# Delta recurrence with its operands exchanged, and masked decays moved to GpSimd

## The chip, the core and the metric

The kernel runs on one core of one Trainium2 chip. A core has five engines that run side by side and meet only at semaphores: TensorE (PE, matrix products, whose weight loads the profile keeps apart as PEld), VectorE (DVE), ScalarE (ACT), GpSimd (POOL) and the queue that starts transfers (SP). The metric is the device time of one execution in microseconds (us); lower is better.

## The reference, cut to what matters

The input is four sequences of 1024 tokens of 128 numbers. First comes one layer of a gated delta recurrence with six heads, keys of 128 and values of 32 numbers:

```python
def step(S, inp):                      # S: batch, head, 128 x 32
    q_t, k_t, v_t, g_t, b_t = inp
    S = S * jnp.exp(g_t)[..., None, None]
    corr = jnp.einsum('bhk,bhkv->bhv', k_t, S)
    u = (v_t - corr) * b_t[..., None]
    S = S + k_t[..., None] * u[:, :, None, :]
    o_t = jnp.einsum('bhk,bhkv->bhv', q_t, S)
    return (S, o_t)
S, o = lax.scan(step, S0, (qt, kt, vt, gt, bt))
```

Behind it come six layers of windowed attention (16 heads of 64, windows of 32 tokens) with a feed-forward block each, all in float32.

## The kernel before, in words

`delta_layer` walks the 1024 tokens in eight tiles of 128, all four sequences (NB = 4) at once. A tile is one block of the program, with a barrier behind it. It first makes projections, convolutions and norms, and then takes the six heads in three pairs; x = 0, 1 is the head of a pair.

The tile's 128 recurrence steps are done as matrices. For a head, k·kᵀ weighted by decays gives a triangular A (`weigh`, into `am`), which TensorE turns (`turn_a`, L384) and ScalarE copies (`take_at`: four copies of 32 rows into `atc`, L638, and a whole one into `at`, L640). The inverse of I + A is doubled block by block in six levels (i = 1 to 6). In each level TensorE makes `first_products`, ScalarE copies them (`p1`, L690 or L694), TensorE makes `second_products`, and VectorE subtracts and turns them (L945, L947; L926 in the last two levels). Between first and second products of levels 1 to 4, TensorE makes the decays and the k·kᵀ, k·q products of the next pair (`decay`, L366 and L367; `products`). A decay reads `gm`, a masked matrix that `masked_decay` on VectorE makes at the start of a pair (L877).

Behind the levels comes what this document calls the pair's closing:

1. `L503`, `L505`: k and q times the state, per sequence one product each; VectorE makes the right side r from them (L972 to L976);
2. `turn_a` for the next pair;
3. `L517`: the inverse (`tt`) times r gives u; VectorE takes it twice (L981, L982);
4. `L525`, `L527`: u times `pm` and times `kt` give the output and the change of the state; VectorE adds both (L990 to L994);
5. `turn_k` for the next pair (L390), which waits for `at`.

The last pair of a tile has no steps 2 and 5. In all products of steps 1, 3 and 4 the loaded operand (the first argument) has 128 columns and the moving one has 32:

```python
pe.matmul(p[3 * x][:, b * DV:(b + 1) * DV], act_qkv[:, H1 + h, s], state[:, h, b, :], start=True, stop=True)
```

`at_block(b)` is the slice of 32 partitions that begins at 32·b. The program gives a product whose operands have 32 or 64 rows or columns a part of TensorE's array; in the trace the form behind the names (`32*32`, `64*32`, `128*128`) is rows by columns of the loaded operand's tile. A float32 product stands in the trace as two records (x2), a turn as one.

`local_layers` is a pipeline over steps g, in an order that is written out for each engine. In VectorE's list `ffn(t, 0)` adds the finished attention output of a tile to `y` (L1581), `sums` reduces squares (L1520), and TensorE's first output product of the next tile (L1287) waits for that addition, since both use one bank.

Of the kernel before, what the change touches and what calls it, by code (L numbers as in the profile page):

```python
# [15 lines left out]
ALU = mybir.AluOpType  # L16
ACT = mybir.ActivationFunctionType
# [121 lines left out]
def delta_layer(nc, sbuf, names, p, y, msk, ident, ones, cst, c, cols, load_done, init_done,  # L139
# [3 lines left out]
    with ExitStack() as ctx:  # L143
# [41 lines left out]
        u = sb("u", [P, 2, 2, NB, DV])  # L185
        o = sb("o", [P, NB, VD])
# [11 lines left out]
        def at_block(n):  # L198
# [20 lines left out]
         on_ready, on_turned, ot_ready, wo_ready, x1_ready, x1_stored) = names(  # L219
            "ks_ready", "r_ready", "u_ready", "u_taken", "o_ready", "s_ready", "o_done", "om_ready",  # L220
            "ostd_ready", "on_ready", "on_turned", "ot_ready", "wo_ready", "x1_ready", "x1_stored")
# [35 lines left out]
        for t in range(-1, NT + 1):  # L257
            attend, behind, ahead = 0 <= t < NT, t >= 1, t + 1 < NT
            LAST_LN, NEXT_LN = 1, 1 + behind
            with nc.Block(no_gpsimd_drain=True) as block:  # L260
# [12 lines left out]
                def _(pe):  # L273
# [119 lines left out]

                    def first_products(pair, i, n):

                        for x in range(2):
                            pe.wait_ge(t_ready, n[x])
                            if i == 1 and pair:
                                pe.wait_ge(r_ready, 2 * pair - 1 + x)
# [26 lines left out]
                    def second_products(pair, i, n):  # L426

                        for x in range(2):
                            pe.wait_ge(p1_taken, n[x])
                            if i == 1 and pair:  # L430
                                pe.wait_ge(u_taken, 2 * pair - 1 + x)
                                pe.wait_ge(s_ready, 2 * pair - 1 + x)
# [7 lines left out]
                            elif i == SMALL:  # L440
                                for b in range(NB):
# [39 lines left out]
                    for pair in range(H1 // 2):  # L481
                        heads = (2 * pair, 2 * pair + 1)

                        for i in range(1, LEVELS):
                            n = [pair * 2 * (LEVELS - 1) + 2 * (i - 1) + x + 1 for x in range(2)]
                            first_products(pair, i, n)
                            if pair + 1 < H1 // 2 and 1 <= i <= 4:
# [12 lines left out]
                        for x, h in enumerate(heads):  # L500
                            for b in range(NB):
                                s = slice(b * P, (b + 1) * P)
                                pe.matmul(p[3 * x][:, b * DV:(b + 1) * DV], act_qkv[:, H1 + h, s],  # L503
                                          state[:, h, b, :], start=True, stop=True)
                                last = pe.matmul(p[3 * x][:, P + b * DV:P + (b + 1) * DV], act_qkv[:, h, s],  # L505
                                                 state[:, h, b, :], start=True, stop=True)
                            last.then_inc(ks_ready, 1)
                        if pair + 1 < H1 // 2:
                            for x in range(2):
                                turn_a(2 * pair + 2 + x)  # L510
                        for x, h in enumerate(heads):
# [4 lines left out]
                            for b in range(NB):  # L516
                                last = pe.matmul(p[3 * x + 1][:, b * DV:(b + 1) * DV], tt[:, x, b, :],  # L517
# [1253 lines left out]
```

## Time and profile before

| | |
|---|---|
| median of 3 runs | 5441.72 us (5439.07 to 5442.9) |
| the profiled execution | 5437.88 us, span 5435.9 us |
| granted TensorE clock, mean | 0.884 |
| busy: PE, DVE, ACT, POOL | 89%, 69%, 51%, 39% of the span |
| one tile of the delta layer | 238.56 us (its `xin` load is issued at 976.25, that of the next at 1214.81) |
| the six local layers | from 1952 us to 5418 us |

The profiled execution lies inside the range of the three runs. A busy share says how long an engine had work in flight, so that TensorE at 89% may still be waiting in places and may be loaded far below its rate in others; which of the two holds in a stretch is read from the timeline of that stretch. The delta layer is the first 14 of the page's 40 slices.

### The profile page before, as it was taken

What the parts mean: (1) busy time and instruction counts of PE and PEld (TensorE: products, weight loads), DVE (VectorE), ACT (ScalarE), POOL (GpSimd) and SP (SyncE); (2) the same over time, 40 slices, a digit from 0 to 9 for tenths busy, and PEclk for the clock granted to TensorE, in tenths of its full rate; (3) what the DMA queues carried; (4) which work ended last, traced back from release to release, by engine and by line L of the source; (5) the groups of instructions that cost most, each with busy time, mean ns of one, the idle gap of its engine ahead of it and who ended that gap; (6) DMA issues with size and microseconds to landing.
All of it is one profiled execution on the core that took longest, in us unless ns stands there. A gap on an engine that the chain in (4) does not pass through costs nothing. (4 is left out here: it accounts for less than half of the span.)

```text
span 5435.9 us, 193069 instructions
## 1 busy us (share of the span) xinstructions
PE 4820.7 (89%) x82128; PEld 3000.6 (55%) x82128; DVE 3747.0 (69%) x6340; ACT 2797.1 (51%) x5325; POOL 2115.8 (39%) x2244
## 2 busy tenths in 40 slices
PE   5867778686777769999999999999999999999997
PEld 3746657474655735555555555555555555555554
DVE  5454554636455468878788888787877888888774
ACT  4243342424334236666666666666666666666664
POOL 2121121212112135555555555555555555555551
PEclk8676776767676669999999999999999999999999
DMA  0000000000000012222222322233222322232222
GB/s 23 4 3 5 2 5 2 5 4 3 6 2 3 2 59 70 67 61 75 73 68 68 82 72 62 64 79 77 68 62 68 79 68 68 74 78 66 59 62 65
DMA packets 255938, 253.45 MB, mean 47 GB/s; under 512 B 29680, under 2 KB 248816, under 8 KB 254704
## 3 DMA queue, kind: packets, MB, share of 16 engines
q1 hardware_dynamic: 255088, 241.09, 17.6%
q8 instruction: 658, 10.78, 0.8%
q14 instruction: 192, 1.57, 0.1%
HBM read 29.71 MB, written 4.19 MB: 6 GB/s over the span
## 5 line engine op out<-in xcount | busy, mean ns | idle before, releaser
L1468 POOL TENSOR_TENSOR turn<-prod 128x512 f32<-128x512 f32 x768 | 982.2, 1279 | 1393.4 <-DVE prod L1508 1371.1
L1205 PE MATMUL banks<-w2s,xs 128*128 128x512 f32 x2304 | 1185.8, 597 | 37.7 <-DVE xs L1541 30.2
L1508 DVE TENSOR_TENSOR prod<-banks,tabs 128x1024 f32<-128x1024 f32 x768 | 940.1, 1224 | 335.2 <-PE banks L1205 322.2
L1477 POOL TENSOR_TENSOR turn<-turn,rs 128x512 f32<-128x512 f32 x768 | 794.8, 1056 | 285.8 <-ACT rs L1371 285.8
L1239 PEld LDWEIGHTS banks<-msk,turn 128*128 128x128 f32 x3072 | 352.5, 140 | 479.8 <-issue 380.6
L1520 DVE TENSOR_REDUCE ss<-sq 128x8 f32<-128x512 f32 x768 | 493.4, 677 | 11.6 <-ACT sq L1353 9.9
L1353 ACT ACTIVATE sq<-banks 128x512 f32<-128x512 f32 x768 | 456.4, 594 | 54.7 <-DVE prod L1508 20.8
L1239 PE MATMUL banks<-msk,turn 128*128 128x128 f32 x3072 | 471.6, 276 | 4.1 <-ACT qt L1386 2.3
L1287 PE MATMUL banks<-ot,w2s 128*128 128x512 f32 x768 | 430.7, 643 | 34.7 <-DVE y L1581 34.0
L1386 ACT ACTIVATE qt<-banks 128x512 f32<-128x512 f32 x384 | 229.2, 597 | 421.5 <-PE banks L1239 420.7
L1384 ACT ACTIVATE kx<-banks 128x512 f32<-128x512 f32 x384 | 229.3, 597 | 407.6 <-PE banks L1239 407.1
L1264 PEld LDWEIGHTS banks<-v,pt 64*32 64x32 f32 x24576 | 269.0, 105 | 289.7 <-ACT qt L1386 141.7
L1393 ACT ACTIVATE pt<-banks 128x512 f32<-128x512 f32 x384 | 229.3, 597 | 324.4 <-PE banks L1246 324.3
L1205 PEld LDWEIGHTS banks<-w2s,xs 128*128 128x128 f32 x2304 | 348.6, 191 | 53.6 <-DVE xs L1541 31.7
L1545 DVE TENSOR_REDUCE mx<-banks 128x8 f32<-128x512 f32 x384 | 263.5, 686 | 130.1 <-PE banks L1225 120.1
L1264 PE MATMUL banks<-v,pt 64*32 64x66 f32 x24576 | 332.5, 225 | 0.2 <-issue 0.2
L1225 PE MATMUL banks<-kx,qt 64*32 64x64 f32 x24576 | 326.0, 222 | 0.0
L1275 PEld LDWEIGHTS banks<-msk,att 128*128 128x128 f32 x1536 | 161.1, 140 | 282.2 <-DVE att L1559 280.6
L1225 PEld LDWEIGHTS banks<-kx,qt 64*32 64x32 f32 x24576 | 299.6, 105 | 0.1
L1314 PE MATMUL banks<-xf,w2s 128*128 128x512 f32 (+1 forms) x576 | 289.8, 616 | 3.1 <-DVE xf L1599 2.8
L831 DVE SCALAR_TENSOR_TENSOR cv<-pre,cw,cv 128x512 f32<-128x512 f32 x336 | 238.3, 781 | 76.9 <-ACT cv L593 71.4
L1559 DVE TENSOR_TENSOR att<-banks,rc 128x512 f32<-128x512 f32 x384 | 265.5, 691 | 13.2
(217 smaller groups left out, 8398.9 us busy)
## 6 DMA issues: line engine op xcount, KB each, us to landing
v<-v_tok SPq DMA_DIRECT2D x1152, 132.0 KB
v<-v_tok SPq DMA_DIRECT2D x384, 66.0 KB
v<-v SPq DMA_DIRECT2D x188, 132.0 KB, 2.5
w2s<-in_weights SPq DMA_DIRECT2D x10, 768.0 KB, 4.9
tabs<-in_rot SPq DMA_DIRECT2D x40, 128.0 KB, 3.2
w2s<-in_weights SPq DMA_DIRECT2D x1, 2713.5 KB, 11.1
w2s<-in_weights SPq DMA_DIRECT2D x10, 256.0 KB, 3.0
xin<-in_x SPq DMA_DIRECT2D x8, 256.0 KB, 2.8
```

The source lines that it names most:

```text
L1205: pe.matmul(a_bank(use), xs[:, t % 2, b * P:(b + 1) * P], w[:, at:at + 512], start=True, stop=True).then_inc(a_done, 1)
L1225: last = pe.matmul(sc[n * WIN:(n + 1) * WIN, h, b * 2 * WIN:(b + 1) * 2 * WIN], qt[r, j, b * P + n * WIN:b * P + (n + 1) * WIN], kx[r, j, ...
L1239: last = pe.transpose(turn_bank[:, i * P:(i + 1) * P], src[:, i * P:(i + 1) * P], ident)
L1264: last = pe.matmul(pv[n * WIN:(n + 1) * WIN, h, b, :], pt[r, g % 2, b * P + n * WIN:b * P + (n + 1) * WIN], v2[r, h2, b, n, i * DV1:(i + 1 ...
L1287: pe.matmul(out_bank, w[:, W_O + j * P:W_O + (j + 1) * P], ot[:, g % 3, :], start=(j == 0), stop=(j == NP2 - 1)).then_inc(o_done, 1)
L1314: pe.matmul(a_bank(n)[0:r, :], w[:, at:at + r], xf[:], start=True, stop=True)\
L1353: a.activation(sq[:, r % 2, :], a_bank(use), ACT.Square).then_inc(sq_done, 1)
L1468: gp.tensor_tensor(turn[:, r % ROTS, :, :].rearrange(halves, s=2), prod[:, r % 2, 0, :, :].rearrange(halves, s=2), prod[:, r % 2, 1, :, :] ...
L1477: gp.tensor_tensor(turn[:, r % ROTS, :, :], turn[:, r % ROTS, :, :], along(rs[:, q % 2, b, :], DH), ALU.mult).then_inc(rot_done, 1)
L1508: v.tensor_tensor(prod[:, r % 2, :, :, :], a_bank(use).rearrange("p (h d) -> p h d", h=HU).unsqueeze(1) .to_broadcast([P, 2, HU, DH]), tab ...
L1520: v.tensor_reduce(ss[:, q % 2, b, :], sq[:, r % 2, :].rearrange("p (h d) -> p h d", h=HU), AX.X, ALU.add).then_inc(red_done, 1)
L1559: v.tensor_tensor(att[:, g % 2, :, :, :].rearrange("p b h n -> p h b n"), pv[:, :, :, 0:DH], rc[:].unsqueeze(3).to_broadcast([P, 2, NB, DH ...
```

## The change

Four things are edited in the delta layer, and one line is moved in the local layers.

- **Exchanged operands.** In steps 1, 3 and 4 the 32-column operand is loaded and the 128-column one moves. The result of sequence b stands in the 32 partitions of `at_block(b)`, turned. ScalarE copies it to SBUF (`kst`, `ut`, `ost`), and TensorE turns it back, all four sequences in one turn. k and q are moved by one product of 256 columns.
- **State products earlier.** k and q times the state are made in level 1, turned back in level 2, and taken by VectorE behind level 3 (`rests`). They need the state of the tile before, and no result of the levels.
- **Masked decays.** Those of heads 2 to 5 are made by POOL, two heads ahead, one instruction of 128 by 512 for a head.
- **ScalarE's copies.** `atc` and `at` are split into `take_blocks` and `take_at`, with the copies of `ut` ahead and those of `ost` between them.
- **Local layers.** VectorE's `ffn(t, 0)` stands ahead of the two `sums` of its step.

```diff
+                    def state_products(pair):
+                        for x in range(2):
+                            h = 2 * pair + x
+                            if pair:
+                                pe.wait_ge(s_ready, h - 1)
+                            for b in range(NB):
+                                last = pe.matmul(p[3 * x + 1][at_block(b), 0:2 * P], state[:, h, b, :],
+                                                 act_qkv[:, h:h + H1 + 1:H1, b * P:(b + 1) * P],
+                                                 start=True, stop=True, skip_group_check=True)
+                            last.then_inc(ks_ready, 1)
+                    def turn_state_products(pair):
+                        for x in range(2):
+                            pe.wait_ge(kst_taken, 2 * pair + x + 1)
+                            for i in range(2):
+                                last = pe.transpose(p[3 * x + 1][:, (2 + i) * P:(3 + i) * P], kst[:, x, i, :], ident)
+                            last.then_inc(ks_turned, 1)
...
                             first_products(pair, i, n)
+                            if i == 1:
+                                state_products(pair)
+                            elif i == 2:
+                                turn_state_products(pair)
...
                             for b in range(NB):
-                                last = pe.matmul(p[3 * x + 1][:, b * DV:(b + 1) * DV], tt[:, x, b, :],
-                                                 r1[:, x, 2, b, :], start=True, stop=True)
-                            last.then_inc(u_ready, 1)
+                                last = pe.matmul(p[3 * x][at_block(b), 0:P], r1[:, x, 2, b, :], tt[:, x, b, :],
+                                                 start=True, stop=True, skip_group_check=True)
+                            last.then_inc(ut_ready, 1)
+                        if pair + 1 < H1 // 2:
+                            for x in range(2):
+                                turn_a(2 * pair + 2 + x)
+                        for x, h in enumerate(heads):
+                            pe.wait_ge(ut_taken, h + 1)
+                            pe.transpose(p[3 * x][:, P:2 * P], ut[:, x, :], ident).then_inc(u_ready, 1)
...
+                                pe.matmul(p[3 * x + 2][at_block(b), 0:P], u[:, x, 0, b, :], pm[:, h % 4, b, :],
+                                          start=True, stop=True, skip_group_check=True)
+                            for b in range(NB):
+                                last = pe.matmul(p[3 * x + 2][at_block(b), P:2 * P], u[:, x, 1, b, :],
+                                                 kt[:, x, b, :], start=True, stop=True, skip_group_check=True)
+                            last.then_inc(ost_ready, 1)
+                        for x, h in enumerate(heads):
+                            pe.wait_ge(ost_taken, h + 1)
+                            for i in range(2):
+                                last = pe.transpose(p[3 * x + 1][:, i * P:(i + 1) * P], ost[:, x, i, :], ident)
                             last.then_inc(o_ready, 1)
...
+                    def masked_decay(h):
+                        g.wait_ge(g_ready, 1)
+                        g.wait_ge(decay_ready, h - 1)
+                        g.tensor_tensor(gm[:, h % 2, :, :], over_batches(gt), along(t24[:, 0, :, h], P), ALU.mult)\
+                            .then_inc(gm_ready, 1)
...
+                            if i == 3:
+                                rests(heads)
...
+                        if 8 <= g and g % 8 == 1:
+                            ffn(g // 8 - 1, 0)
                         if feed:
                             sums(g, 0)
                             sums(g, 1)
-                        if 8 <= g and g % 8 == 1:
-                            ffn(g // 8 - 1, 0)
```

TensorE's order in the closing of a tile's first pair, before (semaphores that a row waits for in brackets):

```order
L503 MATMUL banks<-state,act_qkv 128x32
L505 MATMUL banks<-state,act_qkv 128x32
...
L384 MATMUL banks<-msk,am 128x128 [waits pm_ready,a_ready]
L384 MATMUL banks<-msk,am 128x128 x3
L517 MATMUL banks<-r,tt 128x32 [waits upper_spread,r_ready,lower_spread,tri_ready]
L517 MATMUL banks<-r,tt 128x32 x3
...
L525 MATMUL banks<-u,pm 128x32 [waits pm_ready,kt_ready,u_taken]
L527 MATMUL banks<-u,kt 128x32
...
L390 MATMUL banks<-msk,act_qkv 128x128 [waits at_ready]
L390 MATMUL banks<-msk,act_qkv 128x128 x3
```

and in the changed kernel (L535 is the product for u, L543 its turn, L549 and L552 the products with `pm` and `kt`, L558 their turns):

```order
L535 MATMUL banks<-tt,r 32x128 [waits upper_spread,r_ready,lower_spread,tri_ready]
L535 MATMUL banks<-tt,r 32x128 x3
...
L389 MATMUL banks<-msk,am 128x128 [waits pm_ready,a_ready]
L389 MATMUL banks<-msk,am 128x128 x3
L543 MATMUL banks<-msk,ut 128x128 [waits ut_taken] x2
L549 MATMUL banks<-pm,u 32x128 [waits pm_ready,kt_ready,u_taken]
L549 MATMUL banks<-pm,u 32x128 x3
L552 MATMUL banks<-kt,u 32x128 x4
...
L558 MATMUL banks<-msk,ost 128x128 [waits ost_taken]
L558 MATMUL banks<-msk,ost 128x128
...
L395 MATMUL banks<-msk,act_qkv 128x128 [waits at_ready]
```

The state products have left the closing; each other group keeps its place, and two groups of turns, each behind a copy by ScalarE, have come in.

TensorE's order in level 1 of the first pair of the changed kernel, where the state products (L406) now stand between the first products (L430) and the next pair's decay (L371, L372):

```order
L430 MATMUL banks<-tc,ao 32x32 [waits ao_ready,t_ready]
L430 MATMUL banks<-tc,ao 32x32 x15
L406 MATMUL banks<-act_qkv,state 32x256 x8
L371 MATMUL banks<-msk,gm 128x128 [waits pm_ready,gm_ready,kt_ready]
L372 MATMUL banks<-gm,msk 128x128
```

Eight products of 256 moving columns stand there, where sixteen of 32 stood in the closing.

ScalarE's order in the closing of the first pair, of the changed kernel:

```order
L750 ACTIVATE ut<-banks 128x128 [waits ut_ready] x2
L668 ACTIVATE atc<-banks 32x128 [waits ao_ready,a_turned]
L668 ACTIVATE atc<-banks 32x128 x3
L668 ACTIVATE atc<-banks 32x128 [waits ao_ready,a_turned]
L668 ACTIVATE atc<-banks 32x128 x3
L756 ACTIVATE ost<-banks 128x256 [waits ost_ready] x2
L673 ACTIVATE at<-banks 128x512 [waits a_turned] x2
L685 ACTIVATE kt<-banks 128x512 [waits ktok_ready] x2
```

Before, the copies of `at` stood directly behind those of `atc`, with nothing ahead or between; now `at` stands behind both copies of `ost`.

## Rows read from the trace of the kernel before

**Rows 1.** The page's second part, clock over 40 slices.
```profile
PEclk8676776767676669999999999999999999999999
```

**Rows 2.** Stretches: us, busy PE, PEld, DVE, ACT, POOL (x), PEclk, DMA, GB/s.
```profile
1103.84:1124.40 20.56, 20.56 (x97) 20.23 (x96) 7.79 (x29) 3.82 (x11) 3.48 (x8) 0.50 0.01 1
1124.40:1153.95 29.55, 22.47 (x690) 20.47 (x689) 13.29 (x42) 7.53 (x21) 3.01 (x8) 0.79 0.01 3
```

**Rows 3.** Timeline, first pair's closing: start us, us, instructions, [idle before].
```profile
1103.84 0.63 PE L503 MATMUL banks<-state,act_qkv 128*128 128x32 f32 x2
1103.95 0.42 DVE L926 TENSOR_SCALAR tt<-banks 64x256 f32<-64x256 f32 x1 [0.68 <-PE banks L455]
...
1110.69 1.95 PE L384 MATMUL banks<-msk,am 128*128 128x128 f32 x8
...
1111.82 1.11 ACT L638 ACTIVATE atc<-banks 32x128 f32<-32x128 f32 x4 [9.07 <-PE banks L384]
...
1112.43 3.46 PE L517 MATMUL banks<-r,tt 128*128 128x32 f32 x16
...
1114.22 0.29 DVE L981 COPY u<-banks 128x128 f32<-128x128 f32 x1 [2.17 <-PE banks L517]
...
1115.70 0.61 PE L525 MATMUL banks<-u,pm 128*128 128x32 f32 x2
...
1119.34 0.29 DVE L990 TENSOR_TENSOR o<-o,banks 128x128 f32<-128x128 f32 x1 [0.81 <-PE banks L527]
...
1122.53 1.95 PE L390 MATMUL banks<-msk,act_qkv 128*128 128x128 f32 x8
...
1124.40 1.08 PE L405 MATMUL banks<-tc,ao 32*32 32x32 f32 x64
```

**Rows 4.** Timeline, last pair of the same tile, its closing.
```profile
1193.42 1.97 PE L455 MATMUL banks<-tt,p 64*64 64x64 f32 x16
...
1195.32 0.63 PE L503 MATMUL banks<-state,act_qkv 128*128 128x32 f32 x2
...
1213.23 0.29 DVE L994 TENSOR_TENSOR state<-state,banks 128x128 f32<-128x128 f32 x1
```

**Rows 5.** Timeline, turns and wide products at two clock levels.
```profile
1069.09 1.07 PE L384 MATMUL banks<-msk,am 128*128 128x128 f32 x8 [1.97 <-DVE pm L906]
...
1127.28 0.64 PE L366 MATMUL banks<-msk,gm 128*128 128x128 f32 x2
1127.71 0.63 PE L367 MATMUL banks<-gm,msk 128*128 128x128 f32 x2
```

**Rows 6.** Timeline, local layers, products on 64-row, 32-column tiles.
```profile
3004.82 0.84 PE L1225 MATMUL banks<-kx,qt 64*32 64x64 f32 x64
...
3005.59 1.12 PE L1287 MATMUL banks<-ot,w2s 128*128 128x512 f32 x2
```

**Rows 7.** By line: xcount | busy us, mean ns | idle before, releasers.
```profile
L733 POOL TENSOR_TENSOR sq<-act_qkv 128x512 f32<-128x512 f32 x96 | 109.5, 1149 | 164.6 <-PE banks L356 163.6
L366 PE MATMUL banks<-msk,gm 128*128 128x128 f32 x384 | 107.4, 374 | 59.3 <-DVE pm L906 57.1 <-DVE gm L877 1.1
...
L690 ACT ACTIVATE p<-banks 128x128 f32<-128x128 f32 x240 | 66.6, 278 | 229.2 <-PE banks L405 141.9 <-PE banks L413 83.6
...
L694 ACT ACTIVATE p<-banks 64x256 f32<-64x256 f32 x48 | 18.2, 379 | 61.8 <-PE banks L421 61.4
```

**Rows 8.** Timeline, VectorE inside a doubling level.
```profile
1082.80 0.29 DVE L945 TENSOR_TENSOR tc<-tc,banks 128x128 f32<-128x128 f32 x1 [2.95 <-PE banks L437]
```

**Rows 9.** Timeline, the local layers' step behind a finished tile.
```profile
3013.73 1.10 PE L1287 MATMUL banks<-ot,w2s 128*128 128x512 f32 x2 [0.61 <-DVE y L1581]
...
3016.14 0.63 ACT L1403 ACTIVATE e<-e 128x512 f32<-128x512 f32 x1 [0.24 <-DVE e L1549]
...
3017.46 0.86 PE L1264 MATMUL banks<-v,pt 64*32 64x66 f32 x64
```

**Rows 10.** Group by line, all layers: the output products and their waits.
```profile
L1287 PE MATMUL banks<-ot,w2s 128*128 128x512 f32 x768 | 430.7, 643 | 34.7 <-DVE y L1581 34.0 <-ACT ot L1399 0.7
```

More of the change, by code:

```diff
@@ L185, in delta_layer @@
         u = sb("u", [P, 2, 2, NB, DV])
+        kst = sb("kst", [P, 2, 2, P])
+        ut = sb("ut", [P, 2, P])
+        ost = sb("ost", [P, 2, 2, P])
         o = sb("o", [P, NB, VD])
@@ L500, in _ @@
                         for x, h in enumerate(heads):
[L501 to L511, printed above, removed]
                             pe.wait_ge(tri_ready, h + 1)
@@ L679, in _ @@
                     for h in range(2):
+                        take_blocks(h)
+                    for h in range(2):
                         take_at(h)
@@ L695, in _ @@
                                         .then_inc(p1_taken, 1)
+                            if i == 1:
+                                for x in range(2):
+                                    a.wait_ge(ks_ready, 2 * pair + x + 1)
+                                    a.activation(kst[:, x, :, :], blocks(p[3 * x + 1][:, 0:2 * P], 2), ACT.Copy)\
+                                        .then_inc(kst_taken, 1)
                             if i == SMALL:
@@ L707, in _ @@
                                     rstd(NEXT_LN, p[6])
+                        for x in range(2):
+                            a.wait_ge(ut_ready, 2 * pair + x + 1)
+                            a.activation(ut[:, x, :], p[3 * x][:, 0:P], ACT.Copy).then_inc(ut_taken, 1)
+                        if more:
+                            for x in range(2):
+                                take_blocks(2 * pair + 2 + x)
+                        for x in range(2):
+                            a.wait_ge(ost_ready, 2 * pair + x + 1)
+                            a.activation(ost[:, x, :, :], blocks(p[3 * x + 2][:, 0:2 * P], 2), ACT.Copy)\
+                                .then_inc(ost_taken, 1)
                         if more:
@@ L757, in _ @@
                             last.then_inc(lower_spread, 1)
+                        if pair + 2 < H1 // 2:
+                            g.wait_ge(lower_spread, 2 * pair + 2)
+                            for x in range(2):
+                                masked_decay(2 * pair + 4 + x)
+                    g.wait_ge(gm_ready, H1)
                     g.wait_ge(ao_ready, H1 * (SMALL - 1))
@@ L935, in _ @@
                         more = pair + 1 < H1 // 2
-                        if more:
-                            masked_decay(2 * pair + 2)
-                            masked_decay(2 * pair + 3)
                         for i in range(1, LEVELS):
```

51 lines of the change are left out of this document (26 added, 25 removed).

## The prediction, made before the changed kernel ran

> **What bounds the kernel now.** I read the slices first. The granted clock lies at 5 to 8 tenths in the first 14 slices, which are the delta layer, and at 9 behind them [rows 1]: the two layers have different limits. Next come stretches of one tile of the delta layer (t = 4), taken from its timeline. The closing of its first pair is 20.56 us long and TensorE is busy for all of it, at a granted clock of 0.50; in the levels behind it TensorE is busy for 22.47 of 29.55 us at 0.79 [rows 2]. So in the closing TensorE itself sets the time, and at the lower of its two levels, 1.2 GHz.
>
> Then the timeline of the closing, for what TensorE does there [rows 3]. The sixteen products of step 1 take from 1103.84 to 1110.69, 6.85 us or 0.428 us each. Eight turns take 1.74 us (1110.69 to 1112.43), 0.217 each. The eight products of step 3 end at about 1115.70 (3.27 us), the sixteen of step 4 at 1122.53 (6.83 us), and eight more turns at 1124.40. The price of 0.428 us is the point: the decay's products, which move 128 columns through a full tile, also stand 0.43 us apart at this level (1127.28 to 1127.71) [rows 5]. A product that moves 32 columns and one that moves 128 cost the same, so the loading of 128 columns is what is paid for in steps 1, 3 and 4. The last pair's closing has no turns for a next pair: from 1195.32 until VectorE's last row ends at 1213.52 (1213.23 + 0.29), 18.20 us [rows 4].
>
> **What the exchange does to a product.** Each now loads 32 columns and moves 128 (256 for the state). If products on the four column tiles went one behind the other, each would still cost 0.43 us, by its moving columns. If the four sequences' products run side by side, four cost what one does. No row shows a tile of 128 rows and 32 columns. The nearest are the local layers' score products on tiles of 64 rows and 32 columns: 64 records from 3004.82 until TensorE's next work at 3005.59, 0.77 us [rows 6]. One record that moves 64 columns takes 0.119 us of its tile at the low level (16 records from 1193.42 to 1195.32) [rows 4], so about 0.06 at the full one; 64 of them would take 3.8 us in a row, and 1.9 us if only the two row halves overlapped. They take 0.77: column tiles of one row group do overlap. I take full overlap, 0.43 us for a group of four at the low level, and as the other end no overlap, 1.71 us.
>
> **The closing, worked out anew**, with 1103.84 as zero, at the low level, and about 0.2 us from a product's end to its reader. Head 0's u products run from 0 to 0.43. Head 1's wait for VectorE's last block of `tt`, which starts at 1103.95 and takes 0.42 [rows 3]: 0.65 to 1.08. Eight turns (`turn_a`) run to 2.82. The turns of `ut` follow to 3.26; ScalarE copied it at 0.28 us each [rows 7] before that. VectorE takes u, two instructions like that of 0.29 us [rows 3], which overlap a little, 0.5 us for a head: 3.25 to 3.75 and to 4.25. The products with `pm` and `kt`, two groups of four for a head, run from 3.85 to 4.70 and to 5.56. ScalarE is in `take_blocks` from 2.15 to 4.4 (two times 1.11 us [rows 3]), which is just over before `ost` is ready at 4.9. It copies `ost` at 0.38 us [rows 7], by 5.3 and 6.15. TensorE turns the two at 5.56 to 6.0 and 6.3 to 6.7. ScalarE's whole copies `at` now come behind, about 0.6 us each, to 7.35, so that `turn_k` runs from 6.85 to 8.6, and the next pair's first products begin there. Before, they began at 20.56 (1124.40) [rows 3]. The closing shrinks by 12.0 us. VectorE fits `first_t`, output and state into 4.25 to 8.4, by its rows of 0.29 us [rows 3].
>
> In the last pair the same chain without the turns gives u taken by 2.0 and 2.65, products from 2.15 to 3.87, turns until 5.0, and the state's last row by 6.3, against 18.20: 11.9 us less.
>
> **What comes in elsewhere**, per pair:
> - State products in level 1: two heads, each one group of 256 moving columns, 0.86 us at the low level, 1.7 us in all. TensorE is between `first_products` and the decay there, and ScalarE's copies of `p1` are done before the decay is, so this is on the path. Against it, the levels' clock of 0.79 [rows 2] means that it rises somewhere in them, and it may rise sooner behind the wide products; the turns show what the two levels differ by (eight in 1.07 us [rows 5] against 1.74). I take 1.3 us; the ends are 0.9 and 1.7.
> - Four turns in level 2, 0.87 us at the low level, half at the high one: 0.7.
> - `rests` on VectorE, eight instructions of 0.29 us, 2.3 us. They fall into the idle time of a level, 2.95 us [rows 8]. Nothing, if that cover holds; without it 2.3 us. The levels of the last pair are shorter, and 0.5 us may show there.
> - ScalarE's copies of `kst`, 0.38 us each: beside the decay's products. Nothing.
> - The masked decays: TensorE waited for VectorE's `gm` for 1.1 us in the whole program [rows 7], so their leaving VectorE is worth at most that. On POOL one costs about 1.15 us, by the nearest form, a 128 by 512 product of two operands [rows 7], a pair ahead of its reader. Nothing.
> - Waits that I haven't seen and changes of tile form: 0.5.
>
> So a pair gives 12.0 − 1.3 − 0.7 − 0.5 = 9.5 us. The L366 row counts its products in 384 records, eight for a head [rows 7]: 48 heads, 24 pairs. 24 times 9.5 is 228 us. The profiled execution's 5437.88 us less 228 is 5210; the median of the runs shown stands 3.84 us above that execution, so 5214 us.
>
> **The line moved in the local layers.** TensorE waits 34.0 us in total for the addition at L1581 [rows 10], 0.61 us in the step shown [rows 9]. The addition now comes about 1.2 us earlier and that wait goes. But the step is then VectorE's: its list has the same work up to the subtraction of the maxima, ScalarE's exponent starts only behind that (3016.14, released by VectorE), and TensorE's L1264 at 3017.46 needs a copy that stands behind this exponent [rows 9]. What is late next is the same thing as before. I take 0; the ends are 0 and −34 us.
>
> **The rivals.**
> - *No overlap* (slower). The loads are the reason it could be: the groups load into tiles that share all four row groups. Ten groups of four (four for the state, two for u, four for output and state) cost 1.71 instead of 0.43 us, 12.8 us more in a pair, and 9.5 us less becomes 3.3 more. 24 times 3.3 is 79, so 5521 us. It decides from 1.38 us for a group on (0.43 + 9.5/10), an overlap of less than 1.24. The 64-row tiles speak against it [rows 6]; for it speaks only that no 128-row tile is in the trace. The Trainium skill has this as a rule (TensorE: Matmul & The Clock Gate, Part 3: Packing small matmuls): a weight load overlaps with products in flight only when their row groups differ, and here none do. The score products, with two row groups and 0.77 us for 64 records, don't agree with it as far as it would forbid column tiles; the same part's table measures three column tiles at 2.38 times, which would leave most of the gain, as an estimate.
> - *Half overlap*: 0.85 us for a group, 4.3 us more in a pair, 5.2 us less than before. 5442 − 125 = 5317 us. 64 records in 0.77 us are 12 ns each, so that a limit on issue does not bind groups of eight long records.
> - *The clock rises*. The old closing stood at 0.50 although TensorE was busy throughout [rows 2]; elsewhere in the same tile TensorE does reach the high level, as at the turns at 1069.09 [rows 5]. If the new closing and level 1 run at 2.4 GHz, the turns in the closing cost 0.87 us less twice over, the turns and products 0.8, and the state products and the first decay 1.5: about 3.2 us in a pair at the chain's links that are TensorE's, 77 us in all, 5137 us. Against it: the new closing has gaps at each copy, and half of TensorE's work in it is turns.
> - *The moved line pays in full*: 34 us more, 5180 us.
>
> **How the numbers follow.** Full overlap near the clock of before: 0.60, 5214 us. Clock rises: 0.19, 5137. Half overlap: 0.09, 5317. No overlap: 0.07, 5521. Moved line pays: 0.05, 5180. A measurement of this kernel can tell 0.2%, some 11 us, from no change. Only the case without overlap is slower, and no case but a mixture of poor overlap and lost cover lies within 0.2%: faster 0.92, same 0.01, slower 0.07. The range leaves out the two poor cases (0.16) and a little of the best: below, the risen clock, 5137, with some margin left out of it; above, a pair's gain cut by the uncovered `rests` (2.3) and state products at their dearer end (0.4), 65 us more than 5214. That is 5140 to 5285.
>
> **What would show it.** In the changed kernel's timeline: four products of one head on 128*32 tiles start within some tens of ns, and a group takes about 0.43 us at 0.50; the closing of a first pair is 8 to 9 us long, with ScalarE's copy of `ost` behind `take_blocks` by less than 0.5 us; level 1 is 1 to 2 us longer; no idle time of TensorE is put down to `r` in level 5 or to POOL's `gm`; the local layers' stretch keeps its length while L1287's wait for L1581 is gone. The prediction is wrong if products of one group start one behind the other, if the clock in the closing isn't 0.50, or if levels 1 to 4 grow by more than 3 us.

## The result, and the profile after

The changed kernel takes 5142.47 us (median of 4 runs, 5140.68 to 5147.27) against 5440.93 us for the kernel before beside it (4 runs, 5439.07 to 5442.90). The ratio is 0.9453, with a 95% interval of 0.9436 to 0.9469. It is faster by 298 us. The forecast was 5214, with a range of 5140 to 5285: the time lies inside, at the very low end, and the gain was under-forecast by 72 us.

First the page of the changed kernel: span, busy time by engine and the granted clock in 40 slices.

```profile
span 5138.7 us, 192901 instructions
...
PE 4539.0 (88%) x81984; PEld 2649.1 (52%) x81984; DVE 3693.6 (72%) x6212; ACT 2844.3 (55%) x5469; POOL 2152.4 (42%) x2276
...
PEclk8777777777777899999999999999999999999999
```

Beside [rows 1], the slices of the delta layer all stand at 7 or 8 now, where many stood at 6, and the layer is about a slice shorter. How the time divides is read from the first instruction behind the delta layer, SyncE's load of the key mask. It starts at 1952.26 us in the profile of before. In that of the changed kernel:

```profile
1683.46 0.35 SPq L1167 DMA_DIRECT2D sq<-in_key_mask  x1
```

The delta layer became 268.8 us shorter (forecast 228), and what is behind it, up to the end of the span, 28.4 us shorter: 3483.6 before, 5138.7 − 1683.46 = 3455.2 now (forecast 0). The two add up to the 297.2 us between the spans. So both terms of the forecast were too small, one by 41 us and one by 28.

**The same tile of the delta layer** (t = 4), by stretches, with the columns of [rows 2]: the levels and the closing of the first pair, then those of the second.

```profile
1142.16:1173.28 31.12, 24.09 (x710) 21.10 (x709) 14.31 (x45) 8.29 (x23) 5.65 (x12) 0.77 0.01 3
1173.28:1181.10 7.82, 7.26 (x71) 5.01 (x71) 4.59 (x17) 4.83 (x15) 3.64 (x8) 0.65 0.01 2
1181.10:1211.26 30.16, 23.04 (x710) 20.48 (x709) 14.34 (x46) 8.24 (x24) 3.04 (x9) 0.80 0.01 3
1211.26:1218.87 7.61, 7.09 (x71) 4.87 (x71) 4.41 (x17) 4.83 (x15) 3.43 (x8) 0.67 0.00 0
```

The first pair's closing (second row) takes 7.82 us where it took 20.56 [rows 2]. The forecast had 8.6. TensorE is busy for 7.26 of them, and the clock over the stretch is 0.65, no longer 0.50. The levels of the second pair (third row) take 30.16 us against 29.55 [rows 2], 0.6 more; those of the first pair 1.5 more and those of the last 1.4 more. The forecast had 2.5 more for each pair. Taken over all eight tiles by the same windows, a tile's three closings are together 37.3 us shorter (forecast 35.9) and its levels 3.3 us longer (forecast 7.5).

**The closing in the timeline**, the rows of TensorE, and those of ScalarE and VectorE on which it waits (columns as in [rows 3]):

```profile
1173.28 1.23 PE L535 MATMUL banks<-tt,r 128*32 128x128 f32 x16
...
1174.44 1.97 PE L389 MATMUL banks<-msk,am 128*128 128x128 f32 x8
...
1176.20 0.63 PE L543 MATMUL banks<-msk,ut 128*128 128x128 f32 x2
...
1177.20 0.65 PE L549 MATMUL banks<-pm,u 128*32 128x128 f32 x8 [0.37 <-DVE u L1045]
...
1177.42 0.41 PEld L552 LDWEIGHTS banks<-kt,u 128*32 128x32 f32 x8
...
1178.35 0.38 ACT L756 ACTIVATE ost<-banks 128x256 f32<-128x256 f32 x1 [0.52 <-PE banks L552]
...
1178.95 1.02 PE L558 MATMUL banks<-msk,ost 128*128 128x128 f32 x4
...
1180.02 1.15 PE L395 MATMUL banks<-msk,act_qkv 128*128 128x128 f32 x8
...
1181.10 0.75 PE L430 MATMUL banks<-tc,ao 32*32 32x32 f32 x64
1181.78 1.07 PE L406 MATMUL banks<-act_qkv,state 128*32 128x256 f32 x16
...
1182.78 0.49 PE L371 MATMUL banks<-msk,gm 128*128 128x128 f32 x2
```

The u products of both heads (L535, 16 records for 8 products) go by in 1.16 us, from 1173.28 to 1174.44, where step 3 took 3.27 us. The group with `pm` (L549) starts at 1177.20 and the group with `kt` behind it at 1177.63: 0.43 us for four products on four column tiles, the full overlap of the forecast. The turns at 1174.44 are at the low level (eight from 1174.44 to 1176.20); those at 1180.02 at the high one (eight in 1.08 us, to 1181.10), and so are the state products behind them: two heads in 1.00 us, 1181.78 to 1182.78. In the tile's first pair the same state products run at the low level almost to their end (0.57 over the stretch):

```profile
1143.17 1.77 PE L406 MATMUL banks<-act_qkv,state 128*32 128x256 f32 x16
...
1144.87 0.49 PE L371 MATMUL banks<-msk,gm 128*128 128x128 f32 x2
```

1.70 us, which is two groups of 0.85, the dear end of the forecast's range; and again the decay behind them (L371) is at the high level (its third and fourth product start at 1145.41 and 1145.64, 0.23 us apart).

**Level 1 of the second pair**, its first products and its decay, before and then in the changed kernel, in windows:

```profile
1124.40:1125.41 1.01, 1.01 (x65) 0.94 (x64) 0.93 (x5) 0.88 (x2) 0.00 (x0) 0.50 0.03 8
1125.41:1128.75 3.34, 3.34 (x25) 3.22 (x17) 0.00 (x0) 0.28 (x1) 0.00 (x0) 0.57 0.00 0
```

```profile
1181.10:1181.78 0.68, 0.68 (x65) 0.64 (x64) 0.04 (x1) 0.68 (x3) 0.03 (x1) 1.00 0.00 0
1182.78:1184.77 1.99, 1.99 (x21) 1.87 (x17) 0.00 (x0) 0.48 (x2) 0.00 (x0) 1.00 0.00 0
```

The same work takes 4.35 us before and 2.67 now, at a clock of 1.00. That pays for the state products between the two: with them, level 1 of the second pairs is 4.94 us long in every tile, where before it was 4.1 to 5.6 and 4.9 on average.

**A step of the local layers** behind a finished tile, which answers to [rows 9]:

```profile
2731.90 0.69 DVE L1644 TENSOR_TENSOR y<-banks,y 128x512 f32<-128x512 f32 x1
...
2733.13 1.13 PE L1350 MATMUL banks<-ot,w2s 128*128 128x512 f32 x2
...
2735.93 1.02 PE L1268 MATMUL banks<-w2s,xs 128*128 128x512 f32 x2
2736.21 0.63 ACT L1466 ACTIVATE e<-e 128x512 f32<-128x512 f32 x1 [0.88 <-DVE e L1612]
2736.74 0.58 ACT L1449 ACTIVATE qt<-banks 128x512 f32<-128x512 f32 x1
2736.89 0.86 PE L1327 MATMUL banks<-v,pt 64*32 64x66 f32 x64
2737.68 0.65 PE L1309 MATMUL banks<-msk,e 128*128 128x128 f32 x4
```

The addition (L1644) is over at 2732.59, before the output products (L1350) start, and they wait for nothing. From them the products with `v` (L1327, before L1264) start 3.76 us later, as against 3.73 in [rows 9]: the wait was taken off the front, and nothing came in its place. Over all layers:

```profile
L1350 PE MATMUL banks<-ot,w2s 128*128 128x512 f32 x768 | 432.0, 644 | 0.7 <-ACT ot L1462 0.7
```

The 34.0 us put down to VectorE's addition in [rows 10] are gone.

### The profile page after: what moved, and what is told of

It is laid out like the page before. It is cut to its first block and busy times, and to the rows that moved or that the text cites. A ratio compares the mean times of both kernels' runs of the same rounds, so it can differ in the third digit from the quotient of the medians.

```text
span 5138.7 us, 192901 instructions
## 1 busy us (share of the span) xinstructions
PE 4539.0 (88%) x81984; PEld 2649.1 (52%) x81984; DVE 3693.6 (72%) x6212; ACT 2844.3 (55%) x5469; POOL 2152.4 (42%) x2276
## 5 line engine op out<-in xcount | busy, mean ns | idle before, releaser
L1350 PE MATMUL banks<-ot,w2s 128*128 128x512 f32 x768 | 432.0, 644 | 0.7 <-ACT ot L1462 0.7
L1327 PEld LDWEIGHTS banks<-v,pt 64*32 64x32 f32 x24576 | 270.0, 105 | 290.1 <-ACT kx L1447 107.6
L1327 PE MATMUL banks<-v,pt 64*32 64x66 f32 x24576 | 333.8, 225 | 0.4 <-issue 0.4
```

The lines of the kernel that those rows point to most:

```text
L1327: last = pe.matmul(pv[n * WIN:(n + 1) * WIN, h, b, :], pt[r, g % 2, b * P + n * WIN:b * P + (n + 1) * WIN], v2[r, h2, b, n, i * DV1:(i + 1 ...
L1350: pe.matmul(out_bank, w[:, W_O + j * P:W_O + (j + 1) * P], ot[:, g % 3, :], start=(j == 0), stop=(j == NP2 - 1)).then_inc(o_done, 1)
```

## The experiments

All times are medians; the kernel before ran beside them at 5440.2, 5441.0 and 5437.4 us on the three occasions. Differences "to the changed kernel" are to 5142.47.

### The moved line

**Put back in the changed kernel**, and **moved alone in the kernel before** (the same edit, the other way):

```diff
+                        if 8 <= g and g % 8 == 1:
+                            ffn(g // 8 - 1, 0)
                         if feed:
                             sums(g, 0)
                             sums(g, 1)
-                        if 8 <= g and g % 8 == 1:
-                            ffn(g // 8 - 1, 0)
```

> The changed kernel with VectorE's ffn(t, 0) put back behind the two sums. Theory (TensorE's own list sets the length of that step, so its wait for the addition was paid in full): the local layers' stretch grows from 3455.2 to about 3484 us, the whole to about 5171. Rival (VectorE sets the step, as the prediction had it, and the local layers are shorter for another reason): no change, 5142.

> The kernel before with only the moved line. Theory (TensorE's wait was paid in full): 5441 less 28, about 5413, with no wait of TensorE for the addition left. Rival (VectorE sets the step): 5441. If the delta layer's change were needed for the gain: 5441 too, while putting the line back in the changed kernel costs 28.

Put back: 5174.77 us (5171.01 to 5180.61), ratio to before 0.9513 [0.9499, 0.9527], so the line is worth 32 us there. Alone: 5414.72 us (5413.93 to 5415.35), ratio 0.9953 [0.9938, 0.9968], so 25.5 us. The output products' row with the line back, and then in the kernel before with the line alone moved:

```profile
L1350 PE MATMUL banks<-ot,w2s 128*128 128x512 f32 x768 | 432.7, 645 | 34.4 <-DVE y L1644 33.7 <-ACT ot L1462 0.7
```

```profile
L1287 PE MATMUL banks<-ot,w2s 128*128 128x512 f32 x768 | 432.3, 645 | 1.0 <-ACT ot L1399 0.7 <-DVE y L1581 0.3
```

The wait follows the line in both kernels, and the time follows the wait: 25.5 us is three quarters of the 34, and 32 us over nine tenths. Part of the distance between the two is not the line's. In both profiles the delta layer, which the line doesn't touch, is 4 to 5 us longer than in its partner (the key mask's load starts at 1688.20 and at 1956.52). Behind it, the stretch is 3485.6 us with the line back against 3455.2, and 3455.7 with the line alone moved against 3483.6. By these stretches the line is worth 30 and 28 us, in either kernel, and the two causes are separate.

### Side by side, or one behind the other

**All products of a group on one column tile**, in each of the four groups. The four sequences' results then fall on one another, so that the delta layer's output isn't the reference's; everything else runs as it did.

```diff
-                                last = pe.matmul(p[3 * x][at_block(b), 0:P], r1[:, x, 2, b, :], tt[:, x, b, :],
+                                last = pe.matmul(p[3 * x][at_block(0), 0:P], r1[:, x, 2, b, :], tt[:, x, b, :],
...
```

> The changed kernel with the four sequences' products of every group written to the same 32 partitions, so to one column tile; loads, moving columns, copies and turns stay, and the delta layer's output is wrong. Theory (the gain comes from four column tiles that run side by side): ten groups per pair at four times their length, 12.8 us more per pair at the low level and 6.4 at the high one, 24 pairs: 5300 to 5450 us, near the time of before. Rival (the gain comes from loading 32 columns in place of 128, and from the order): under 60 us more, 5200.

5274.39 us (5273.99 to 5275.21), ratio 0.9695 [0.9679, 0.9711]: 132 us more than with four tiles, 5.5 us for each of the 24 pairs. That is between what the two theories had. The products did go one behind the other (16 records in 3.54 us, 1262.25 to 1265.79, where four tiles take 1.16):

```profile
1229.86 4.47 PE L406 MATMUL banks<-act_qkv,state 128*32 128x256 f32 x16
...
1262.25 3.60 PE L535 MATMUL banks<-tt,r 128*32 128x128 f32 x16
1265.79 1.09 PE L389 MATMUL banks<-msk,am 128*128 128x128 f32 x8
1266.71 0.38 PE L543 MATMUL banks<-msk,ut 128*128 128x128 f32 x2
```

But behind them the turns run at the high level (eight in 0.92 us), and so does all that is left of the closing. The window over it, in a fence of its own:

```profile
1262.25:1273.29 11.04, 10.41 (x72) 8.38 (x71) 4.99 (x17) 4.83 (x15) 3.47 (x8) 0.84 0.01 1
```

11.04 us at a clock of 0.84. Without any overlap the new closing is still 9.5 us shorter than the old one of 20.56 [rows 2]. Of these, 6.85 us are the state products, which have left the closing; in level 1, on one tile, they take 4.40 us (1229.86 to 1234.26). The kernel is 166 us faster than before. So the overlap of the tiles carries 132 us, about half of the delta layer's 269, and the other half stands without it. That half needs another cause, and the clock column names one.

### The clock, by itself

**The kernel before, with 128 columns moving in place of 32** in each product of steps 1, 3 and 4. The loads, their number and the order of work stay; each product moves the columns of all four sequences, four times the work, into a place that the next one overwrites, so that the delta layer's output is another one.

```diff
-                                pe.matmul(p[3 * x][:, b * DV:(b + 1) * DV], act_qkv[:, H1 + h, s],
-                                          state[:, h, b, :], start=True, stop=True)
+                                pe.matmul(p[3 * x][:, 0:P], act_qkv[:, H1 + h, s],
+                                          flat4(state[:, h, :, :]), start=True, stop=True)
...
```

> The kernel before, in which each product of steps 1, 3 and 4 moves the columns of all four sequences (128 in place of 32) and the four write the same place; the loads, their number and the order stay, and the delta layer's output is wrong. Four times the moving work, nothing taken away. Theory (at 0.43 us the products are paid by their loads or their moving columns alike at 1.2 GHz, and what keeps the closing there is that so little moves through the array): the granted clock rises within the closing, as it did in the run with one column tile, so that of 40 products and 16 turns all but the first 8 or so cost half: about 8 us less per pair, 5240 to 5290 us. Rival (the clock of a closing has nothing to do with what moves): 0.50 in the closings as before, 5441 us.

5263.54 us (5261.69 to 5265.47), ratio 0.968 [0.9666, 0.9695]: four times the columns moved, and 174 us less. Its closing in a window, and in TensorE's timeline:

```profile
1059.92:1072.44 12.52, 12.52 (x98) 12.35 (x97) 6.91 (x25) 3.56 (x11) 3.65 (x8) 0.86 0.01 1
```

```profile
1062.21 0.64 PE L509 MATMUL banks<-state,act_qkv 128*128 128x128 f32 x2
1062.64 0.63 PE L507 MATMUL banks<-state,act_qkv 128*128 128x128 f32 x2
1063.07 0.55 PE L509 MATMUL banks<-state,act_qkv 128*128 128x128 f32 x2
1063.45 0.39 PE L507 MATMUL banks<-state,act_qkv 128*128 128x128 f32 x2
1063.67 0.39 PE L509 MATMUL banks<-state,act_qkv 128*128 128x128 f32 x2
```

The same number of products now stands in 12.52 us at a clock of 0.86, with TensorE busy throughout as before. They start 0.43 us apart up to 1063.07, and 0.22 from 1063.45 on: the clock rises while step 1 runs. With 32 columns it never rose in 20.56 us of the same busy engine [rows 2]. This holds in every tile: in the sixteen closings of a first or second pair the clock is 0.50 each time before, and 0.82 to 0.86 here. The old closing was long because its narrow products held TensorE at 1.2 GHz, and not only because each paid for a load.

In this run and in the one before it the delta layer computes on other numbers. That the numbers alone move the clock wasn't tried. The next two runs and the changed kernel speak against it: they compute what the reference does, and the clock stays at 0.50 in the narrow products of those two, while it reaches 1.00 in the changed kernel's closing (1178.95 to 1181.10).

### Which exchange brings what

**States early, but in the old narrow form** (k and q loaded, 32 columns moving), with the rest as changed:

```diff
-                                last = pe.matmul(p[3 * x + 1][at_block(b), 0:2 * P], state[:, h, b, :],
-                                                 act_qkv[:, h:h + H1 + 1:H1, b * P:(b + 1) * P],
...
+                                pe.matmul(p[3 * x + 1][:, 3 * P + b * DV:3 * P + (b + 1) * DV],
+                                          act_qkv[:, H1 + h, s], state[:, h, b, :], start=True, stop=True)
...
```

> The changed kernel with the state products early, in level 1, but in the old form (k and q loaded with 128 columns, the state's 32 moving, no copy and no turn). Theory (price by loaded columns, 0.43 us each at the low level and about 0.22 at the high one, sixteen of them in line on TensorE, against 1.0 to 1.7 us for the exchanged ones and 0.5 for their turns): 2 to 5 us more per pair, 5190 to 5260. Rival (the early place hides them in either form): 5142 to 5155.

5244.66 us (5239.13 to 5248.50), ratio 0.9638 [0.9623, 0.9652], 102 us more than the changed kernel, 4.3 a pair. Its timeline at the end of these products:

```profile
1216.02 0.61 PE L407 MATMUL banks<-state,act_qkv 128*128 128x32 f32 x2
1216.44 0.61 PE L409 MATMUL banks<-state,act_qkv 128*128 128x32 f32 x2
1216.87 0.78 PE L371 MATMUL banks<-msk,gm 128*128 128x128 f32 x2
1217.44 0.63 PE L372 MATMUL banks<-gm,msk 128*128 128x128 f32 x2
1217.86 0.63 PE L371 MATMUL banks<-msk,gm 128*128 128x128 f32 x2
```

Sixteen products from 1210.02 to 1216.87, all 0.43 us apart, and the decay behind them stands at 0.43 us too, where behind the wide state products it stood at 0.22. The narrow products cost their own time (6.85 us, where the wide ones take 1.70 or 1.00) and, behind them, part of that of others.

**u and output in the old form**, states exchanged and early:

```diff
-                                last = pe.matmul(p[3 * x][at_block(b), 0:P], r1[:, x, 2, b, :], tt[:, x, b, :],
-                                                 start=True, stop=True, skip_group_check=True)
-                            last.then_inc(ut_ready, 1)
+                                last = pe.matmul(p[3 * x][:, P + b * DV:P + (b + 1) * DV], tt[:, x, b, :],
+                                                 r1[:, x, 2, b, :], start=True, stop=True)
+                            last.then_inc(u_ready, 1)
...
```

> The changed kernel with steps 3 and 4 in the old form (tt, pm and kt loaded, 32 columns moving, no ut and ost copies, no turns), the state products exchanged and early. Theory (narrow products keep the closing at 1.2 GHz, 0.43 us each): closing about 20.56 less 6.85, 13.7 us against 7.8, so 5 to 6 us per pair, 5260 to 5285. Rival (the closing's gain is mostly the removal of the state products, 6.85 us): two copies by ScalarE and two groups of turns are saved, 5150 to 5200.

5288.25 us (5282.87 to 5291.94), ratio 0.9723 [0.9706, 0.9739]: 146 us more than the changed kernel, 6.1 a pair, slightly over the upper end of what was expected. Its closing in a window:

```profile
1092.05:1105.78 13.73, 13.73 (x65) 13.40 (x64) 5.16 (x17) 3.83 (x11) 3.71 (x8) 0.50 0.00 1
```

13.73 us, TensorE busy for all of it, the clock at 0.50: the old picture again, in a closing without the state products, and so in all sixteen closings of this kind.

**State products and their turns put back into the closing**, exchanged as in the change; `rests`, and ScalarE's copies of `kst`, with them:

```diff
-                            if i == 1:
-                                state_products(pair)
-                            elif i == 2:
-                                turn_state_products(pair)
...
+                        state_products(pair)
+                        turn_state_products(pair)
```

> The changed kernel with the exchanged state products, their copies, turns and VectorE's rests back in the closing, behind level 6. Theory (the early place hides the chain of copy, turn and VectorE's 2.3 us, and costs only TensorE's part in levels 1 and 2): closing some 5 to 6 us longer, levels about 1.5 shorter, 3.5 to 4.5 us per pair, 5225 to 5250. Rival (the exchange alone makes the gain, the place is worth nothing): 5142 to 5165.

5198.71 us (5191.84 to 5203.82), ratio 0.9555 [0.9541, 0.957]: 56 us more, 2.3 a pair, between the two expectations. The u products now wait for VectorE's r:

```profile
L532 PE MATMUL banks<-tt,r 128*32 128x128 f32 x384 | 29.6, 394 | 29.1 <-DVE r L991 29.1
```

In their early place the state products, their copies, turns and `rests` lie beside the levels' other work; here they stand in a row ahead of the u products. Over the eight tiles the closings became 93 us longer, by windows of both profiles, and 29.1 of these are the waits of this row; the levels, without these products, became 34 us shorter.

### The decays on POOL, and ScalarE's order

**Masked decays back on VectorE**, all heads, and **the `at` copies with their blocks as before**:

```diff
-                    for h in (2, 3):
-                        masked_decay(h)
...
+                        if more:
+                            masked_decay(2 * pair + 2)
+                            masked_decay(2 * pair + 3)
```

```diff
                             for x in range(2):
                                 take_blocks(2 * pair + 2 + x)
+                                take_at(2 * pair + 2 + x)
...
-                            for x in range(2):
-                                take_at(2 * pair + 2 + x)
```

> The changed kernel with the masked decays of heads 2 to 5 back on VectorE at the start of a pair. Theory (VectorE idles for over 4 us in level 1 and TensorE needs the first of them only behind the state products): within 5 us of the changed kernel, 5137 to 5147. Rival (with the shorter closing VectorE comes late to the pair's start): 1 us for each of 16 pairs, about 5158.

> The changed kernel with ScalarE's whole copies at beside their block copies again, so ahead of the copies of ost. Theory (ost is waited for on the path, and two copies of 0.6 us stand before it in the closings of the first two pairs of a tile): about 1.1 us for each of 16 closings, 5160. Rival (turn_k behind it waits for at anyway, so the order is worth nothing): 5142.

5145.23 us (5140.65 to 5147.35), ratio 0.9455 [0.9441, 0.9469], and 5138.36 us (5136.76 to 5142.29), ratio 0.9444 [0.943, 0.9458]. Neither can be told from the changed kernel. The first agrees with the forecast's nothing. The second was expected to cost 18 us. It contradicts the forecast's closing, in which `ost` and its turns were on the path and the late `at` copies were there to keep it short: put first, they cost nothing.

### A version that beats both

What was still idle in the levels is TensorE between a level's second products and the next level's first, and in level 3 its wait for `pm` (on L371: 2.57 us at a time, 56.9 us in the program with that at the start of a tile). **The next pair's decays and products, split**: the first two sequences' between a level's two products as before, the other two behind its second ones:

```diff
-                                (decay, products)[(i - 1) % 2](2 * pair + 2 + (i - 1) // 2)
+                                fill, of = (decay, products)[(i - 1) % 2], 2 * pair + 2 + (i - 1) // 2
+                                if i != 3:
+                                    fill(of, range(2))
...
                             second_products(pair, i, n)
+                            if pair + 1 < H1 // 2 and 1 <= i <= 4:
+                                fill(of, range(2, NB) if i != 3 else range(NB))
```

and then **the turns of the state products behind level 2's second products**, with the `at` copies beside their blocks:

```diff
-                            elif i == 2:
-                                turn_state_products(pair)
...
                             second_products(pair, i, n)
+                            if i == 2:
+                                turn_state_products(pair)
```

> The changed kernel, where TensorE makes the next pair's decays and products half between first and second products and half behind the second products (in level 3 all of it behind). Theory (in levels 1 to 4 TensorE is the engine that sets the time except while VectorE subtracts and turns, 1.2 us a level, and while it waits 2.6 us for pm in level 3): the work behind the second products fills both, 2 to 3 us for each of 16 pairs, 5095 to 5110. Rival (ScalarE's copies or the lower clock take it back): 5142.

> The kernel with the next pair's products split over both gaps of a level (5070 us), and with the turns of the state products behind level 2's second products and ScalarE's copies at beside their block copies. Theory (turns fill VectorE's part of level 2, too, 0.4 us for each of 24 pairs, and the copies' order is worth nothing or some us): 5055 to 5065. Rival (level 2 is full already): 5070.

5070.46 us (5068.14 to 5071.33), ratio 0.9318 [0.9302, 0.9333], 72 us less than the changed kernel, more than was expected; and 5055.29 us (5054.49 to 5056.75), ratio 0.9298 [0.9284, 0.9312], 87 us less. The second is the fastest kernel of this study; its two edits weren't told apart, and the kernel before ran 3.6 us faster beside it than beside the first. For the first, the row that answers to the wait for `pm`:

```profile
L372 PE MATMUL banks<-msk,gm 128*128 128x128 f32 x384 | 96.3, 339 | 29.8 <-DVE pm L975 28.4 <-DVE gm L946 1.2
```

28.4 us in place of 56.9. That is 28.5 of the 72; the rest lies in the levels, and was not taken apart.

## Why the prediction was right, and where its steps were wrong

**Right: what a group costs.** Full overlap on four column tiles, 0.43 us for a group at the low level, as the rows at 1177.20 and 1177.63 show. The Trainium skill (TensorE: Matmul & The Clock Gate, Part 3: Packing small matmuls) has a weight load overlap only when the row groups differ. Here the groups share all four, and the measurement decides against that rule: the loads of the group with `kt` (L552, 1177.42 to 1177.83) lie inside the products of the group with `pm` (1177.20 to 1177.85), two heads' state products took 1.70 us on four tiles, and 16 records of the u products 1.16 us, against 3.54 us on one tile.

**Right: the shape of the new closing.** Its chain held link by link. `turn_k` was foreseen to start 6.85 us behind the closing's first product and started at 6.74 (1173.28 to 1180.02). The last pair's closing was foreseen at 6.3 us and took 6.5, from 1241.07 until VectorE's last row at 1247.54. The cover of `rests` held: no idle time of TensorE is put down to `r`. POOL's decays are worth nothing, as priced.

**Mis-sized: the clock, in the closing and more so in the levels.** The forecast took the low level throughout the closing and left the risen clock to a rival with 0.19 and 77 us. Its own sign of being wrong, a clock in the closing that isn't 0.50, came true: 0.65. The 41 us by which the delta layer's gain was under-forecast, about half of what that rival had, lie in two terms.

- The closings, 12.0, 12.0 and 11.9 us less in the sum, became 12.7, 12.9 and 11.7 us shorter (means over the eight tiles): 11 us in the program. Most of it is the last link, the eight turns of `turn_k`, which take 1.08 us at the high level and not 1.74.
- The levels were summed at 2.5 us more for each pair (state products 1.3, turns 0.7, unseen 0.5) and became 1.6, 0.8 and 0.9 longer: 34 us in the program. The state products themselves took 1.70 us in the first pair, the dear end of the range, and 1.00 at the high level in the second. But the decay behind them went from 2.75 to 1.98 us in the first pair and from 3.34 to 1.99 in the second, and the second pair's first products from 1.01 to 0.68. So level 1, foreseen 1 to 2 us longer, became 0.7 longer in the first pairs and 0.1 in the second.

The two come to 45 us; the rest of the delta layer gave 4 back. So the likeliest case and this rival were both partly true. I took the old closing's 0.50 as given, though TensorE was busy throughout, and did not ask what in it kept the clock down, nor what a risen clock would do to the work behind. Four times the moving columns in the old closing raised it to 0.86 and made the kernel 174 us faster, with every load as before; narrow state products in level 1 put the decay behind them at 0.43 us a product, in the pair shown above. These runs show the cause. The rival's own price doesn't add up as it stands: its links come to 4.0 us a pair and 3.2 are counted, without saying which are left out.

**Wrong for the same reason: the price of the rival without overlap.** It was put at 5521, slower than before. Measured, that case is 5274, 166 us faster than before: with one tile the closing ran at 0.84, and a group of four took 0.87 us there (1268.47 to 1269.34), not 1.71. The 0.07 for slower stood on the low level, which the products did not keep to.

**Failed: the step on the moved line.** "TensorE's L1264 at 3017.46 needs a copy that stands behind this exponent" was a claim about the order of two instructions, which I didn't check in the code. These products take the `pt` of the step before: in the changed kernel it is copied at 2730.91, and the products run at 2736.89. What does need the exponent is the turn of `e` (L1309), which comes 0.84 us after the exponent's end (2736.84 to 2737.68). So TensorE's own list set the step, VectorE's and ScalarE's parts had room, and a wait taken off TensorE came back as time: 28.4 us between the profiles, 30 and 28 in the stretches of the two experiments, of the 34.0 that the row promised. The rival with 34 us was the true one and had a chance of 0.05.

**What the shares are.** Undone one at a time, u and output exchanged are worth 146 us, the states exchanged 102, the line 32: 280 of the 298, each with what the clock does to the work behind it. They are no exact division: the early place of the states, undone alone in the wide form, is worth 56. What stays open is how the 132 us of the tiles' overlap and the effect of the clock interact within a pair, as every edit that lengthens the products also changes the clock behind them.

## What to carry to other kernels

A stretch in which TensorE is busy throughout at a granted clock of 0.50 need not be at its limit, as these closings weren't: look at how many columns its products move, and try to exchange loaded and moving operands where the loaded side is the wide one. Price such a change at both clock levels, and the work behind it too, for products 0.43 us apart may be followed by turns at half or at full speed depending on what went ahead. Before a wait is called "replaced by the next one", find in the code which instruction, of which step, the next wait is for, and measure its slack.

## What the runs showed of the hardware

- Products that moved 32 columns behind loads of 128 kept the granted clock at 0.50 for 20.56 us with TensorE busy all the time; the same products moving 128 columns started 0.43 us apart at first and 0.22 from the tenth on, and the closing fell to 12.52 us. Wide moving made the program 3.2% faster with four times the columns moved.
- At 1.2 GHz a product in fp32 behind a load of 128 columns cost 0.43 us with 32 and with 128 columns moving, so that the narrow form had nothing to offer in exchange for the clock that it cost.
- Four column tiles of 128 rows and 32 columns ran fully side by side: 0.43 us for four products of 128 moving columns at 1.2 GHz, about as much as one such product took where all eight of both heads used one tile (3.54 us, clock 0.51), and 0.85 for four of 256 (clock 0.57).
